# One attention layer written anew: context attention with keys on partitions, bfloat16 products for the maximum, and its input norm by chunks

## What is computed

```python
def _L1_xattn_ref(x, y, wq, bq, wk, bk, wv, bv, wo, bo):   # x 2x1024x256 (normalised), y 2x64x192
    q = (x @ wq + bq).reshape(B, Sq, H, D).transpose(0, 2, 1, 3)      # H = 16 heads of D = 16
    k = (y @ wk + bk).reshape(B, -1, H, D).transpose(0, 2, 1, 3)      # 64 keys
    v = (y @ wv + bv).reshape(B, -1, H, D).transpose(0, 2, 1, 3)
    scores = jnp.einsum('bhqd,bhkd->bhqk', q, k) / jnp.sqrt(jnp.asarray(D, x.dtype))
    attn = jax.nn.softmax(scores, axis=-1)
    out = jnp.einsum('bhqk,bhkd->bhqd', attn, v)
    out = out.transpose(0, 2, 1, 3).reshape(B, Sq, E)
    return out @ wo + bo
...
x = x + _L1_xattn_ref(_layernorm(x, axis=-1), ctx_768, L1_xattn_wq, ...)
```

## Time and profile before

| | us |
|---|---|
| median of 3 runs | 1726.46 |
| the profiled execution, whole | 1722.57 |
| its span | 1720.9 |
| PE busy | 1575.2 (92%) |
| DVE busy | 969.3 (56%) |
| ACT busy | 727.1 (42%) |
| POOL busy | 351.8 (20%) |

### The profile page before, as it was taken

The page is one execution under the profiler, slowest core; times in us unless marked ns, Lnnn a source line. Parts: engine busy times, 40 slices in busy tenths (PEclk is TensorE's granted clock), DMA queues, the critical chain, the costliest instruction groups (busy, mean ns, idle before and its releaser), DMA issues. The chain is left out here.

```text
span 1720.9 us, 19851 instructions
## 1 busy us (share of the span) xinstructions
PE 1575.2 (92%) x7202; PEld 886.8 (52%) x7202; DVE 969.3 (56%) x1539; ACT 727.1 (42%) x1280; POOL 351.8 (20%) x280
## 2 busy tenths in 40 slices
PE   6889999989998999878999997799779999999997
PEld 3644444422222244343545443366357888888885
DVE  4742133766767532248777762466458665574752
ACT  3344123533334342523665663323335554545441
POOL 0000000132122100323000000000204655655551
PEclk9989999998999999988999999899889999999998
DMA  6000000000000000073443200000301222222201
GB/s 263 1 1 0 0 0 4 1 1 1 0 1 1 0 0 0 1 146 38 112 64 50 38 2 4 0 1 0 123 0 66 96 73 95 78 86 77 87 9 50
DMA packets 38709, 67.55 MB, mean 39 GB/s; under 512 B 3864, under 2 KB 19288, under 8 KB 38232
## 3 DMA queue, kind: packets, MB, share of 16 engines
q1 hardware_dynamic: 38616, 66.33, 14.7%
HBM read 57.80 MB, written 8.39 MB: 38 GB/s over the span
## 5 line engine op out<-in xcount | busy, mean ns | idle before, releaser
L1943 ACT ACTIVATE arena<-psum 128x512 f32<-128x512 f32 (+3 forms) x384 | 164.7, 501 | 123.4 <-PE psum L1833 91.2
L1994 DVE TENSOR_REDUCE b_mx<-psum 128x1 f32<-128x512 f32 (+3 forms) x304 | 181.3, 654 | 45.5 <-PE psum L1811 34.5
L2470 POOL TENSOR_TENSOR m_w_rest<-m_w,m_w_high 128x512 fp32r<-128x512 f32 (+1 forms) x88 | 111.8, 1272 | 177.5 <-ACT m_w_high L2651 177.5
L2880 DVE TENSOR_TENSOR m_hidden<-m_gelu,psum 128x512 f32<-128x512 f32 (+1 forms) x88 | 60.4, 686 | 147.1 <-ACT m_gelu L2727 122.9
L2555 PE MATMUL psum<-m_x_high,m_w_high 128*128 128x512 f32 (+1 forms) x352 | 137.9, 392 | 2.9 <-issue 2.9
L2555 PE MATMUL psum<-m_x_rest,m_w_high 128*128 128x512 f32 (+1 forms) x352 | 137.7, 391 | 0.0
L2555 PE MATMUL psum<-m_x_high,m_w_rest 128*128 128x512 f32 (+1 forms) x352 | 137.6, 391 | 0.0
L2476 POOL TENSOR_TENSOR m_h_rest<-m_hidden,m_h_high 128x512 fp32r<-128x512 f32 (+1 forms) x88 | 121.9, 1385 | 58.5 <-ACT m_h_high L2665 58.5
L1196 ACT ACTIVATE x_probs<-psum 128x1024 f32<-128x1024 f32 x64 | 65.6, 1025 | 137.2 <-PE psum L948 137.2
L1339 DVE TENSOR_REDUCE x_mx<-psum 128x2 f32<-128x1024 f32 x64 | 77.0, 1220 | 54.3 <-PE psum L922 54.1
L2727 ACT ACTIVATE m_gelu<-psum 128x512 f32<-128x512 f32 (+1 forms) x88 | 52.6, 598 | 119.5 <-PE psum L2555 119.5
(11 more groups left out here) (505 smaller groups left out, 3086.7 us busy)
## 6 DMA issues: line engine op xcount, KB each, us to landing
m_w<-w SPq DMA_DIRECT2D x32, 512.0 KB, 4.6
m_wo<-wo SPq DMA_DIRECT2D x16, 512.0 KB, 3.9
weights_sb<-weights SPq DMA_DIRECT2D x2, 2820.0 KB, 12.2
m_w<-w SPq DMA_DIRECT2D x16, 344.0 KB, 4.7
b_q_stack<-b_q_dram SPq DMA_DIRECT2D x36, 128.0 KB, 6.8
b_k_stack<-b_k_dram SPq DMA_DIRECT2D x36, 128.0 KB, 7.2
weights_sb<-weights SPq DMA_DIRECT2D x1, 3328.0 KB, 13.3
b_q_dram<-b_q_parts SPq DMA_DIRECT2D x6, 512.0 KB, 3.7
```

The lines of the kernel that those rows point to most:

```text
L1943: act.activation(probs[slot % RING][:, 0:n], score(slot)[:, 0:n], ACT.Exp, scale=SCALE).then_inc(s["expd"].sem)
L1994: dve.tensor_reduce(mx[:, part, qi, heads[0]:heads[0] + nh], tile(("piece", p))[:, 0:nh * keys].rearrange("p (h n) -> p h n", n=keys), AX, ...
L2470: pool.tensor_tensor(w_rest[:, n % W_RING, :, :, 0:H_N(n % HT)], raw_of(n), w_high[:, n % W_RING, :, :, 0:H_N(n % HT)].bitcast(F32), ALU.s ...
```

## The change

The fifth layer becomes one block without the loop. A unit is 512 tokens of one half of the features (8 heads), eight units in all, (b, j, m). In it:

- The scores are made with keys on the partitions: `k_pair` holds two heads' 64 keys, and a product takes 32 rows (two heads of 16 features, the other one's rows being zero for each half of the columns). Two such products, in two row groups of 32, fill the two banks of a score tile; two tiles (`scores(2u)`, `scores(2u+1)`) make a unit. Before each pair goes a bfloat16 product of 32 rows that subtracts the head's maximum.
- The maximum is taken from products of its own, in bfloat16, tokens on the partitions (`maxima`): 32 of them, eight ahead of the units and four beside each of units 0 to 5, in a ring of two banks that projections and shifts share. After each eight of them (four tiles of 128 tokens, both halves of the features) the maxima are rounded, transposed and copied (`split_shift`, `turn_shift`, `keep_shift`).
- exp reads PSUM and writes SBUF (ACT, 128 x 1024, 16 of them). Nothing is transposed after it.
- `values(u)` makes the sum for each head with a matrix of ones (4 products in four column groups) and then the output (4 products in four column groups), keys on the contracted side. DVE takes a reciprocal of 128 x 512 and multiplies.
- q is rounded to bfloat16 by POOL. The bias of the values is folded into the last addition.
- The norm of chunks 0 and 1 moves into the last two half steps (`hs` 14 and 15) of the fourth layer; of chunks 2 and 3 the sums are made at that layer's very end, and the rest at the start of the fifth.
- A bfloat16 identity is made once at the start instead of in two layers.

```diff
+    def next_norm(hs, ki, x):
+
+        if hs >= HALVES - 2 and ki in (1, 2) and x == 2:
+            return [("mean" if hs % 2 == 0 else "var", ki - 1)]
+        return []
...
+                    if hs == HALVES - 2 and ki == 3 and x in (2, 3):
+                        ch = x - 2
+                        act.wait_ge(*s["read"](nth["mean", ch] + 1))
+                        act.wait_ge(*s["later_part"](4))
+                        act.activation(next_squares(ch), chunk(xn_all, ch), ACT.Square).then_inc(yn["sq"].sem)
+                    if hs == HALVES - 1 and ki == 4 and x == 0:
+                        for ch in (0, 1):
+                            act.wait_ge(*s["read"](nth["var", ch] + 1))
+                            act.activation(next_factor(ch), next_factor(ch), ACT.Ln, bias=c.eps[:, 0:1]).then_inc(yn["log"].sem)
+                        for ch in (0, 1):
+                            act.wait_ge(*yn["log"](ch + 1))
+                            act.activation(next_factor(ch), next_factor(ch), ACT.Exp, scale=-0.5).then_inc(yn["rstd"].sem)
...
+                for ch in LATE:
+                    next_sum(ch)
...
+    def beside(u):
+
+        out = []
+        if u < 6:
+            b, t = divmod(2 * u + 4, TT)
+            out += [("max", b, t + i, m) for i in (0, 1) for m in range(FT)]
+            if u % 2:
+                out.append(("shift", b, t // 4))
+        if u in (3, 5, 7):
+            out += [("project", *unit(u - 3)[:2], m) for m in range(FT)]
+        return out
...
+                def scores(x):
+                    u, half = divmod(x, 2)
+                    b, j, m = unit(u)
+                    if half == 0 and m == 0:
+                        pe.wait_ge(*s["read"](nth["shift", b, j] + 1))
+                    if x >= 2:
+                        pe.wait_ge(*s["expd"](x - 1))
+                    elif half == 0:
+                        pe.wait_ge(*s["q_raw"](8))
+                    rows = [slice((2 * half + i) * 2 * DH, (2 * half + i + 1) * 2 * DH) for i in (0, 1)]
+                    for i in (0, 1):
+                        pe.matmul(score(x)[:, i * CH:(i + 1) * CH], of_pair[rows[i], 2 * half + i, m].rearrange("p i n -> p (i n)"),
+                                  shift_t[rows[i], (NCH * b + j) % 2, :], start=True, stop=False)
+                    for i in (0, 1):
+                        mm = pe.matmul(score(x)[:, i * CH:(i + 1) * CH], k_pair[rows[i], b, m, :], q[b][rows[i], m, col(j)],
+                                       start=False, stop=True)
+                    mm.then_inc(s["scored"].sem)
+
+                def values(u):
+                    b, j, m = unit(u)
+                    pe.wait_ge(*s["expd"](2 * u + 2))
...
+                        pe.wait_ge(*s["normed"](u))
+                    for to, of in ((den_tile, lambda r: ones[:]), (out_tile, lambda r: v_pair[:, b, r, :])):
+                        for i in range(QUADS):
+                            mm = pe.matmul(to[i * 2 * DH:(i + 1) * 2 * DH, :], of(QUADS * m + i), probs[(2 * u + i // 2) % RING][:, i % 2, :],
+                                           start=True, stop=True)
+                        mm.then_inc(s["av"].sem)
...
+                for u in range(UNITS):
+                    scores(2 * u)
+                    if u >= 1:
+                        values(u - 1)
+                    scores(2 * u + 1)
+                    for what in beside(u):
+                        make[what[0]](what)
+                values(UNITS - 1)
+                for what in order[-FT:]:
+                    project(what)
...
+                def normalise(u):
+                    b, j, m = unit(u)
+                    dve.wait_ge(*s["av"](2 * u + 1))
+                    dve.reciprocal(den_inv[:], den_tile).then_inc(s["den_inv"].sem)
+                    dve.wait_ge(*s["den_inv"](u + 1))
+                    dve.wait_ge(*s["av"](2 * u + 2))
+                    dve.tensor_tensor(ot[b][:, m, col(j)], out_tile, den_inv[:], ALU.mult).then_inc(s["normed"].sem)
...
+                for u in range(UNITS):
+                    if u >= 1:
+                        normalise(u - 1)
+                    for what in beside(u):
+                        if what[0] == "max":
+                            maxima(what)
+                        elif what[0] == "shift":
+                            split_shift(what)
+                            keep_shift(what)
+                        else:
+                            finish(what)
+                normalise(UNITS - 1)
```

More of the change, by code:

```diff
@@ L1871, in project, with early_norm @@
                     mm.then_inc(s["made"].sem)
+                def early_norm(what):
+                    kind, ch = what
+                    to = tile(what)
+                    if kind == "mean":
+                        pe.wait_ge(*yn["sum"](ch + 1))
+                        mm = pe.matmul(to, c.mean_w[:], next_factor(ch), start=True, stop=True)
+                    else:
+                        pe.wait_ge(*yn["sq"](ch + 1))
+                        for k in range(FT):
+                            mm = pe.matmul(to, c.mean_w[:], next_squares(ch)[:, k, :], start=(k == 0), stop=(k == 1))
+                    mm.then_inc(s["made"].sem)
                 def more_pieces(first, last):
@@ L1895, in _ @@
                         project(0, x)
+                    for what in next_norm(hs, ki, x):
+                        early_norm(what)
                 values(len(groups) // 2 - 1)
@@ new lines, in tile, with maxima @@
+                def tile(what):
+                    n = nth[what]
+                    if n >= 2:
+                        pe.wait_ge(*s["read"](n - 1))
+                    return ring_bank(what)
+                def maxima(what):
+                    _, b, t, m = what
+                    to = tile(what)
+                    if t % 4 == 0 and m == 0:
+                        pe.wait_ge(*s["rounded"](4 * b + 2 * (t // 4) + 2))
+                    pe.matmul(to, q16[b][:, m, t * P:(t + 1) * P], k_diag[:, b, m, :], start=True, stop=True).then_inc(s["made"].sem)
@@ new lines, in project @@
+                def project(what):
+                    _, b, j, m = what
+                    to = tile(what)
+                    pe.wait_ge(*s["normed"](FT * (NCH * b + j + 1)))
+                    for k in range(FT):
+                        mm = pe.matmul(to, c.w("y_wo", k, m * P, P), ot[b][:, k, col(j)], start=(k == 0), stop=(k == 1))
+                    mm.then_inc(s["made"].sem)
+                make = dict(max=maxima, shift=turn_shift, project=project)
+                for ch in LATE:
+                    pe.wait_ge(*yn["sum"](ch + 1))
+                    pe.matmul(norm_bank(ch), c.mean_w[:], factor(ch), start=True, stop=True).then_inc(yn["mean"].sem)
@@ new lines, in _ @@
+                pe.wait_ge(*g["keys"](2))
+                pe.wait_ge(*g["bias"](1))
+                pe.wait_ge(*g["vd"](1))
+                for what in first_tiles[:-1]:
+                    maxima(what)
+                pe.wait_ge(*yn["out"](4))
+                for n in range(4):
+                    query(1, n)
+                turn_shift(first_tiles[-1])
+                pe.wait_ge(*g["pairs"](2))
+                for u in range(UNITS):
[5 more added lines that the diff above has]
+                        make[what[0]](what)
@@ new lines, in finish @@
+                def finish(what):
+                    _, b, j, m = what
+                    x = chunk(c.xT, 2 * b + j)[:, m, :]
+                    dve.scalar_tensor_tensor(out=x, in0=tile(what), scalar=bias[:, m:m + 1], in1=x, op0=ALU.add, op1=ALU.add)\
+                       .then_inc(s["read"].sem)
+                for ch in LATE:
+                    dve.wait_ge(*yn["mean"](ch - 1))
+                    for k in range(FT):
+                        ins = dve.tensor_tensor(chunk(xn_all, ch)[:, k, :], chunk(c.xT, ch)[:, k, :], norm_bank(ch), ALU.subtract)
+                    ins.then_inc(yn["cent"].sem)
```

412 lines of the change are left out of this document (215 added, 197 removed).

## The result

| | before | changed |
|---|---|---|
| median | 1726.53 us (4 runs) | 1702.27 us (4 runs, 1700.05 to 1705.40) |
| ratio | | 0.9859, 95% interval 0.9841 to 0.9876 |
| profiled run, span | 1722.57, 1720.9 | 1703.28, 1701.5 |
| granted clock, whole span | 0.958 | 0.956 |

The account below looks back on a forecast made before the run. It took PE to bound the batches before and an alternating DVE-PE chain after: 116.7 for the fifth layer, 8.0 + 1.4 + 0.4 at the fourth's end, 16 for the clock, 142.5 against 155.2, so 1713.8 us, range 1696 to 1738.

Parts of the forecast that it names:

- The layer at full clock: Fifth layer's new chain, summed step by step from one reciprocal's start to the next: 116.7 us with its start.
- rival 3: Score products: row groups of 32 don't run side by side, 10.9 us more on the chain, 1724.7 us; chance 0.08.
- The loss of 0.3 us for a score tile: Score tiles: possible extra at the skill page's 3.07 times for four row groups, some 3 us over the chain.
- six steps of 2 us and 4 in the start: Fifth layer: cost of PE's clock falling in the steps with maxima and in the start, 16 us.
- 39.9 + 4: Fifth layer's start, to the first reciprocal: 39.9 us at full clock, plus 4 for the low clock.
- my 12.7: Whole kernel: the gain forecast, 142.5 against 155.2 us, giving a median of 1713.8 us.
- Rival 1: PE's clock holds through the fifth layer: gain 28.7 us, 1697.8 us; chance 0.17.
- Rival 2: PE's clock stays low nearly throughout the fifth layer: price up to 57 us, 1754.8 us; chance 0.14.
- The fourth layer: Its price for the early norm: roots 5.2, squares 1.0, mean and variance products 1.8, sum 8.0 us.
- all 5.2 count: Fourth layer: ACT's ln, exp and table loads delay all later exps and PE waits, so 5.2 us count in full.
- eight reciprocals alone being 26.8: Fifth layer: DVE is on the chain for about 55 us, 26.8 of it the eight reciprocals.
- POOL's casts, ACT's exps, additions at nothing: Fifth layer: sign of being wrong altogether, if one of these, costed at nothing, sets the steps.

Follow-up runs that it names:

- e10: The first two maximum products of a step issued five times each from the second unit on, against the changed kernel: 1699.90 us, beside 1704.41 for that kernel.
- e8: Both score products of a tile take the same group of 32 rows, count and size unchanged, against the changed kernel: 1726.34 us.
- e12: The four sum products, and the four value products, of a unit all write the same 32 rows of their bank, against the changed kernel: 1728.21 us.
- e1: The fourth layer's two ln and two exp moved behind its last copy, their multiplications behind its last bias additions, against the changed kernel: 1696.71 us.
- e2: The norm of chunks 0 and 1 put back from the fourth layer into the fifth, against the changed kernel: 1703.16 us.
- e4: The eight reciprocals of 128x512 left out, a constant multiplied instead, against the changed kernel: 1687.30 us.
- e3: Units reordered against the changed kernel: PE's sums ahead of later maxima, score tiles adjacent, DVE's maxima before the reciprocal, shift's copy after it: 1698.05 us.

## Why the prediction was right, and where its sizes were off

**The layer at full clock: right.** My sum for units and last projections was 76.8 us (11.1, 2 x 8.4, 2 x 14.0, 5.4, 6.7, 8.8). The kernel with its clock held (e10) has 76.36. Piece by piece: 11.68, 7.97, 13.06, 7.97, 13.07, 5.35, 6.67, 10.59. That the sums agree to 0.4 is partly luck. The two steps with projections were 0.9 too dear each and the two with maxima alone 0.4, 2.7 in all. A part of it is that I took each maximum at 0.71 where they start 0.60 apart: 0.2 for the two maxima on the chain of a step with maxima alone, 0.4 for the four of the others. The first step was 0.6 and the tail 1.8 too cheap. The tail runs to the expert layer and holds projections of which part ran at 1.2 GHz even here. The "84 us of units" in the clock's paragraph isn't this sum either; 76.8, or 85.2 with the step that belongs to the start, would be.

**Side by side, rival 3: refuted.** e8 and e12 show what the groups are worth. The price I gave rival 3, ten tiles of 1.09 on the chain, 10.9 us, was too low by half: it left out the clock. With rows that don't run side by side the change is worth nothing, as I said, but by another sum. The loss of 0.3 us for a score tile, given beside the prices, did not come either: a pair takes 0.95 us to the next kind.

**The clock: the term that was mis-sized.** I took six steps of 2 us and 4 in the start, 16 us. Filling PE's pauses gave 6.3 in the profile's units and 4.5 in the medians. My rule that every step with maxima begins low was wrong: the clock swings, but by step the loss was 0.8, 0, 2.4, 1.2 and 1.7, and nothing in the two steps without maxima. For the start I had 39.9 + 4; it took 40.8 behind the late sums, barrier included, so 3.1 less; no run says how much of its 40.8 is clock. These 5.7 and 3.1, less the 1.9 that the fourth layer paid more, make 6.9 of the 8.3 by which the profiles' 21.0 beat my 12.7. The units' sum at full clock gives 0.4, the barrier that the 40.8 already holds 0.4, and 0.5 is that my window of 155.2 us stopped before the expert layer's first work (1222.40 for 1222.89). By the medians the gain is larger still, 24.3 or 22.3. The mean clock in the units, 0.83, lay just above my 0.6 to 0.8.
On the Trainium skill's page "TensorE: Matmul & The Clock Gate", section "A second HAM failure mode: psum-queue depth-cycling": the trace agrees with it, since the clock swings in the units (mean 0.83), and with the pauses beside the reciprocals filled it stays at 0.96 (e10). The section gives no price, and I had let it speak for mine.

**Rival 1, the clock holds: not what happened**, as the clock is 0.83; but by the medians the time, 1702.27, lies nearer to its 1697.8 than to 1713.8. **Rival 2, clock low throughout: no.** e8 shows how near it is, though: 0.73 and no gain with PE's scores twice as long.

**The fourth layer: 8.0 forecast, 9.9 paid.** Roots 5.1 as said (5.2). e1 leaves 2.7 for squares and products, my 1.0 + 1.8. The missing 2 us go with the clock behind the roots: "all 5.2 count" stopped at PE's wait and forgot what a wait of 5.14 us does to PE's next products. The last exp ended 38.3 us behind the anchor for 28.3, 10 later where I had 8. I had also not asked whether the early norm pays at all. It doesn't (e2).

**DVE on the chain: right in kind.** The distance of each reciprocal from the next was taken as DVE's row plus PE's part, and it is. But "eight reciprocals alone being 26.8" reads as if that were what they cost; e4 gives 18.4 in the profile and 15.0 in the medians, and at a clock that is held either way 12.2, since PE works beside them.

**POOL's casts, ACT's exps, additions at nothing: no sign against it.** ACT is busy for 13.2 and POOL for 0.02 of 82.6 us of units, and each reciprocal waits for PE's sums. No run leaves one of them out.

## What to carry to other kernels

When two engines hand work to and fro through a ring of two banks, write both engines' rows beside each other and ask of every short instruction that the other waits for whether something long stands ahead of it. Here a copy of 0.4 us that stood behind a reciprocal of 3.4 rather than before it cost 3.3 us in the one pair of steps where nothing else moved, and it stood there three times. Put small products of different row groups next to each other: two score tiles side by side took PE 1.20 us, one alone 1.17. And price a wait of TensorE twice: once as time, once as the clock behind it; a saving on TensorE that only makes it pause is no saving (the bfloat16 maxima), and a unit of waste on it can come back doubled (the shared rows).

## What was unexpected of the hardware

- Four fp32 products of 512 columns in four column groups take 0.88 us to the next kind, one after another 3.45: 3.9 times. Two in two row groups of 32: 1.02 for 1.88, 1.8 times. The Trainium skill's page "TensorE: Matmul & The Clock Gate", section "Part 3: Packing small matmuls — row/col tiling", has 3.07 times for four row groups. Here four fp32 products in four row groups take 0.97 us to the next kind (e3, 1122.90 to 1123.87), for four of 0.87 one after another: 3.6 times, more than the page has.
- Reducing 512 columns takes DVE 0.68 us in groups of 64 and 0.69 in groups of 128, but behind each other such instructions start every 0.60 us.
- Forty added products left PE's busy time where it was (61.2 for 61.5 us).
- Leaving out eight reciprocals of 3.36 us gave 18.4 us, of which 6.2 go with TensorE's clock.
